# Macaron block on one core: the opening's stage order searched anew, up to about tile 13

## What is computed

```python
def _L0_ffn_ref(x, gate_w, w1, w2, w3):
    xf = x.reshape(-1, orig_shape[-1])
    scores = jnp.einsum('td,ed->te', xf, gate_w)
    probs = jax.nn.softmax(scores.astype(jnp.float32), axis=-1)
    weights, idx = jax.lax.top_k(probs, TOP_K)
    weights = weights / jnp.sum(weights, axis=-1, keepdims=True)
    x1 = jax.nn.silu(jnp.einsum('td,efd->tef', xf, w1))
    x3 = jnp.einsum('td,efd->tef', xf, w3)
    out_all = jnp.einsum('tef,edf->ted', x1 * x3, w2)
    expert_outs = jnp.take_along_axis(out_all, idx[:, :, None], axis=1)
    result = jnp.einsum('tkd,tk->td', expert_outs, weights)

x = x + 0.5 * _L0_ffn_ref(_layernorm(x), gate_w, w1, w2, w3)
x = x + _L0_attn_ref(_layernorm(x), W_q, W_k, gain, bias, log_mix, log_scale)
x = x + 0.5 * _L0_ffn_ref(_layernorm(x), gate_w, w1, w2, w3)
```

## Time and profile before

| | |
|---|---|
| three executions | 804.45, 806.5, 806.85 us; median 806.5 |
| the profiled execution | span 805.2 us from its first to its last instruction; the page gives no other time for it |
| TensorE busy | 695.8 us |
| VectorE, ScalarE, GpSimd busy | 561.3, 501.8, 451.6 us |
| granted TensorE clock, mean | 0.950 |

### The profile page before, as it was taken

How to read it: one execution, slowest core, us unless ns; L and a number is a source line. 1 busy time by engine, 2 the same in 40 slices (tenths; PEclk the granted TensorE clock), 3 DMA queues, 4 the chain that set the end, 5 groups by cost and what they waited for, 6 DMA issues and landing times.

```text
span 805.2 us, 17412 instructions
## 1 busy us (share of the span) xinstructions
PE 695.8 (86%) x4632; PEld 429.6 (53%) x4632; DVE 561.3 (70%) x1599; ACT 501.8 (62%) x975; POOL 451.6 (56%) x545
## 2 busy tenths in 40 slices
PE   1751458999999999999988999998999889999992
PEld 1641225566555665665555656655665555665652
DVE  6679782333687887889879898898865624335766
ACT  4647743353579895967779798977866324334431
POOL 3467878544443446567566645774676656453232
PEclk9875689999999999999999999999999999999997
DMA  8967476868796987888999898788988888699998
GB/s 337 426 221 162 116 211 179 164 134 143 170 206 126 180 159 149 199 160 172 168 171 197 173 192 168 149 186 135 186 158 178 162 201 144 128 164 212 236 246 320
DMA packets 318614, 150.75 MB, mean 187 GB/s; under 512 B 299133, under 2 KB 302589, under 8 KB 317757
## 3 DMA queue, kind: packets, MB, share of 16 engines
q1 hardware_dynamic: 300637, 111.98, 67.4%
q0 software_dynamic: 17888, 37.65, 16.7%
HBM read 33.96 MB, written 44.81 MB: 98 GB/s over the span
## 4 chain that ended last, share of the span: by engine, by line
PE 48%; DVE 18%; DMA 10%; issue 9%; ACT 6%; SPq 5%; POOL 3%; another core or an unknown queue 1%; POOLq 0%; ACTq 0%; DVEq 0%
PE B L1247 28%; PE B L1263 16%; DVE t_W L1557 2%; DMA yt<-t_W,t_idx 2%; DMA t_ph<-t_p 2%; DMA hs<-t_s,t_POS 2%; POOL hs L960 2%; DMA t_gh<-t_gp 2%; DVE t_s L1614 2%; DVE t_th L1755 1%; DMA t_W<-t_W 1%; PE B L1315 1%; PE B L1276 1%; SPq L1052 1%; DVE t_X L1775 1%
## 5 line engine op out<-in xcount | busy, mean ns | idle before, releaser
L1247 PE MATMUL B<-t_W,t_ht 128*128 x1704 | 398.9, 383 | 22.4 <-DVE t_W L1557 7.1
L1247 PEld LDWEIGHTS B<-t_W,t_ht 128*128 128x128 f16 x1704 | 166.8, 99 | 200.7 <-issue 35.8
L1755 DVE SCALAR_TENSOR_TENSOR t_th<-B,t_K,t_th 128x512 f32<-128x512 f32 x142 | 105.7, 747 | 115.9 <-PE B L1247 90.8
L1008 POOL DMA_INDIRECT yt<-t_W,t_idx x107 | 112.5, 1052 | 119.8 <-ACT t_W L1405 71.8
L1263 PE MATMUL B<-t_W,t_gh 128*128 x1284 | 160.7, 276 | 9.4 <-issue 6.4
L960 POOL DMA_INDIRECT hs<-t_s,t_POS x112 | 116.0, 1035 | 63.0 <-issue 29.0
L1263 PEld LDWEIGHTS B<-t_W,t_gh 128*128 128x128 f16 x1284 | 125.0, 99 | 43.2 <-issue 13.7
L1389 ACT ACTIVATE t_th<-B,t_K 128x512 f32<-128x512 f32 x142 | 96.8, 683 | 76.8 <-PE B L1247 49.1
L1398 ACT ACTIVATE t_gp<-t_th 128x512 f16<-128x512 f32 x107 | 66.2, 624 | 48.3 <-DVE t_th L1755 40.1
L1000 POOL DMA_DIRECT2D t_idx<-hs x142 | 80.1, 569 | 24.0 <-DMA yt<-t_W,t_idx 13.4
L1766 DVE TENSOR_TENSOR t_gp<-t_th,t_gp 128x512 f16<-128x512 f32 x107 | 75.0, 707 | 26.1 <-ACT t_gp L1398 21.3
(11 more groups left out here) (214 smaller groups left out, 898.2 us busy)
## 6 DMA issues: line engine op xcount, KB each, us to landing
t_W<-wk SPq DMA_DIRECT2D x6, 2048.0 KB, 17.6
t_hp<-yt SPq DMA_DIRECT2D x16, 512.0 KB
t_s<-yt SPq DMA_DIRECT2D x15, 512.0 KB
t_X<-x SPq DMA_DIRECT2D x8, 512.0 KB, 7.4
out<-t_X SPq DMA_DIRECT2D x7, 512.0 KB
t_ht<-hs SPq DMA_TRANSPOSE x142
t_idx<-hs POOLq DMA_DIRECT2D x142, 0.5 KB
hs<-t_ph SPq DMA_DIRECT2D x2, 952.0 KB, 5.0
```

The lines of the kernel that those rows point to most:

```text
L1008: eng.indirect_dma_start(yt_d[L], bass.IndirectOffsetOnAxis(ap=IDX[:, n % RING:n % RING + 1], axis=0), YO[n % YR], None).then_inc(d_y[n % ...
L1247: t = eng.matmul(B[b][:], HT[n % HTR][:, (2 * hl + db) * 128:(2 * hl + db) * 128 + 128], W16[:, bass.ds(expert[n] * 4096 + (db * 2048 + wl ...
L1755: eng.scalar_tensor_tensor(out=th[:], in0=B[b1][:], scalar=K[:, 7:8], in1=th[:], op0=ALU.mult, op1=ALU.mult).then_inc(free[b1], 1)
```

## The change

Only the string `ORDER` is changed: its first 459 stages, up to `ids 13`, `high 13` and the up halves of tile 14, are arranged anew; the 2662 behind them stand in the same order. The set of stages is the same, and so is each kind's own order but for `scatter`, `mark` and `rexp`. Since the three banks for the up halves are handed out in the order, they come to be permuted for all later tiles.

```diff
 ORDER = (
-    "))Bt)%)Bztf%efYeKY())BYY))BttLKL$$KLKL%$$++++qx%wpfeYKvY!!))fDLKL$$++eYYKLKL$++$Bt-^!!%f^!!e++>)q++xwp)Bt^+++++^"
-    "!!)YYz==+%)B??vV++++:$+ufe=Y=Y??t:$::%=?=?==!!fe^!!!^^!))?=B?$$=_!tY__Yqx??w==WW::uW??=p=+v$$%!1fe^!1!1!1?z?==Y^"
-    "^?Y:=:??==??;.;>;=N$^.?$S;qx!w~~~>;;.pP==!!uWWvD>-[~;NNSWQ}S.Whh??=?P!!1!1P^1QhVQ!1^1^=?M;W>;;|!1!1.NSs1>;~~.^E;"
-    "|>FNPyEN!1hQ!1|_SPuQ~^F;!1;!E>|.;SFE.F*PNW~;>;SQNPE.;>FE_~**W~SNSWP;.s1;>N;;S~uWQQWPca.FNS>;.;EQWW>F_;E~*Ns1FS*;"
+    "))Bt))%Bzt%f(eYfY))BeKLKYYtL)$%$KLK$L$)Btf)+)++%f+Bqx+wept%efv+YY++DKY!LK+!Y!$L$KLKLe++^!^^!$$!))++B-t++q!xY^:V+"
+    "wzp%Y:v=+++=++f!)?!)e?B+YY!=$$=?+?==?=u^!t!!+^?!:=):)^?=BW!Wu>W$%$qfxwpeY?tvY%Wz?=:$fe!1_:?!1$YY=?^=?~:$=?^^==?="
+    "?!1!1!1=^?:$q;x;!w>p!u.;!v^D?.!1!1;>NS=NS-[?!1^;;WW.N>s3P=PS!1h=?;?=?P^!1V.^;>;.;>NN=?!1;==??;.>N^!1!s1WSP;QS.;W"
+    ">QPEF!|QW||SP|~}NQS;EFP;hhE*>Qh;_.FE~y*___N*F~~Q.~u~~~*;EFEMN~WWS>;P_W._FSP*WuQQ*;NSP>;Wc.;>;;.>;.N;>NaSEs1WN~~F"
...
```

More of the change, by code:

```diff
@@ L133 @@
[L133 to L152, removed]
@@ new lines @@
+    "UU))BXF;;.>;QE*;~~t.WQuFWNS%IS>fNPPEe*YYJJW;;.S>;;>NUUUQ.PFU;;>))NBS.PTTWWW~*~~~~~QNEt%mFSonm&on/*___;Wu}Q;>Qf.P"
+    "<#;.&#NZ/E&#;GiSF~j<SeEW/Z<GFblYP&#ZYibGTj/N>;;>E.d;;>lTQP<CdNZi*_~*jmCl.GF~bobnmoSiA_E&n/*j;;ANF<SWW>PuPl#*dZ.&"
+    ";C/AQQQGQd~CA<i#SZEGFNjP*&;>OEWl/QW#&;r)b.FSiN)BSPPj;E#>;<t%.FfNJJUWWuSU.*;EP>;;>NQe.SWl/bZ;<PYFZU.GiQd;GEd>UNj*"
+    ")*;Q;_~C1Y:)Btb%l$F>NS.iNPEjFdQC:W*feE;l;bFSSYYP$ETTPqC>.Nxw;FE.QdCWF;N>puv*A1WQWSS~Amonmo&;;n#>P/P*A;*A_*&Or.<Z"
+    "/N.!GiE<^FQWQW;#WNZQ>;;>j~~~~~!!)&~ESSGPP.^/lQuW<N)#;FZ.iB;>&GSj/l<ENFSi!#ZG;;>~~.Ed1Pt%Pb1FfJJjUUd**N;;UU))S**."
@@ new lines @@
+    "b1PQEBtC1~A>;;>WlWWFi*b1.eEjYYd;QQFbC1EN%C.lWQ;d>SfeA1P;F.~YC*A1:NEFS:;YT*T$ENPSP*A$N>F;S.Oqx;Ewpv!r!N))BWtQPm>;"
+    ".onm~;>;~&SFEoP^%.Qu;f!n/~~~>#&<NN/ZQW;;>F^e#.!&*~~YYuWQJ;WW;>WN:JGiUU;ESPS.S<F#j/PlPQZ;$N.><E;***dZG&#GWF:iQQbU"
+    "U))BtjSul.E;P%*Ffe*$N/NW>qxYE;FC<.SAYw;>TTiEbjd;lp*F*S;P.QEZGWCviPNN!jmonmb1Fo&n/l~EQAQQSb#WF<d&!>ZCAd/^Gi<C;AjP"
+    "&SP.l;#>#;/O^ZN!Qr))!~Gi;>Bt**~~~d<jZ&/b.%EWWFSCfNJe;*E;>;WlJPUdY.F*Q;Y:UNbSGEUF.s2CU)P)B:uQ>;E*F#$i~NtjE$;>%.s<"
+    "FSfqEFexwsP;YpAQlWQvE;.**!!bFSZGiDA>dYPNS^TTCNEj;;>m.oW!^!-nlPmQ;;>bdASVNsoPFy1nC&S.E/AQ&F#uQWWWNP/<O<S**_~E#&r)"
@@ new lines @@
+    ")BZt;.;>;;>.NSF~**;EP%feJJ.uWWQWQ_NUPUYYSF;>;#;>E.UUNPG)ZSF;)ijNB;__E::.*G>$/*F<tPQQ;lWu$&E%fbqxZFw;>SQWijeNYEFp"
+    "G#**d;lPCEAY/b1..d;~<T>;*NvQSSFiENTS!ZjbGCPFPWmo~~~nmon&/lib;>;.jQWQ&#<.sN/;EZS^<P!Al#dNGiPCZ*j>&;Fd#WuG**.E/<Sb"
+    "CQlW&Zy2Q;>#AFi~~~^;dPAjO/yWlu<rZNGi)!j*WC)BGQ~~_lE;F.N>;d!ES;~~t~P*bb1>%FC;i.jEbfJWJUWUNUl.e;>dYN;;SPCSFS.dU**A"
+    "1AA>NCP)QW)BA*y1S;;Y.tEON:%uQ$>;;WQP:.Qr))WPNBtFf>;;e_ES.>YYFSPN;$;TT.E>;;F>P%Nfeqxw.QWWuWWQYEF***mYponv&mSSEon/"
+    "P~F~_*<~!;NPD&#::QQ.Z~~~!G;#>;;>E/&-S.^$;#$i!~b~PN~Wj<Z^FE!*NS;/.PqlQVF<Gi>;ZNdExw&;>pG.FSjCEPSAQWl#/biFjN*b<~;;"
@@ new lines @@
+    ".QZdSQ_C_*N**luGSi>EF;;WA~d>EPv.QjPFl;;>CENS.NSPPdbW;W;>;QWu**~FAC*.ANPO~~~WEQQQWr));.F>;N!~*BtES;>;SF!E.P%fWWeF"
+    "^NuY;>;.NYESF_;!EQPP.>;SP*FN::QW.;*^!>;N$$q**.SP;SE>;~;xwpQN.NFPWWvEQuQW~_S*PFS>;.;>D~N~~!*~~E;;>;F^E.P.S-[FEWWQ"
+    "NPQ;NSP*!^WQ|Vhhh!*|>E;;.NF!|Whu|*_F>;;Q>SQPEEQ.*NFSWP;.F;>;N._;EFEFE**QNWuWW>;;WSP~__S~__.NESPPS>;FF;.NPQSP_***"
+    "~~~~~~~~~QWQQ*~~>;.;>E;;WE>WN.SFPNSQQu;;>.FW*NSPP;.;>EF;NS;E>;.NS~~~**~F*~_;.WQWWPQEQuNP>;FE.FS**~~~;N>;;EE.>;PS"
+    "Fs;NSP~E*F*~PQW>;u.NSF*y1PQWE.F*~;>N~~EFSPQQ;EFWQW;>;.NS.;*PNSPQWuEEFF>;;>;.NSPQQWW;.NS~QEFEE~W***~P>;;>;FQF~**."
@@ L159 @@
+    "*N.;NSPSP>;;>E.NWJJ;;UUUF.SPNUJJWWQ>;;.NU~~Q~EF>;;SPUUUSJEu.WWs1NFQPy>;*.;SNS>E;;>JPU.EsQFFUUNSUWQPy1JQW;EgJEW;."
+    ">QP*UNS*F;;.>;;NS.PUPNuWEQQ>;;>W.F;;*>F**UUSNSPJPEEJg;]1QQ.NSUUUUg1.;FF']J*E*~NPg1yE,FFS]],**EEFF],P**g'EF]***'E"
+    "F*JUUUUJJUUUUJJJUUggUUggg")
 class Plan:
```

7 lines of the change are left out of this document (2 added, 5 removed).

## The result

The changed kernel took 808.64 us (median of 20 runs, 803.45 to 813.43), the kernel before 804.61 us (20 runs beside them, 799.1 to 811.57). The ratio is 1.0056, 95% interval 1.0038 to 1.0073: slower by some 4 us, where 798.0 and "faster" were forecast. The profiled execution had a time of 807.4 us, a span of 805.7 (before: 805.2) and a mean granted clock of 0.950.

What follows compares the result with a forecast made beforehand. GpSimd's queue up to the last fill was taken to set TensorE's hand-over at down 5; GpSimd and ScalarE's chain end together near 133, gaining 8.5 us: 798.0 from 806.5. Range 793.5 to 807; the forecast's own 794 to 800.5.

Steps and rivals of the forecast that it cites:

- Start of group 0, group 1 and group 2: GpSimd's first scatters of these groups: sooner by 1.3, 6.0 and 6.1 us, from earlier positions on VectorE.
- From group 2 to the last fill: GpSimd's stretch: six ids leave (minus 3.4 us), places 0 enters (1.0); last fill at 129.0, gain 8.5.
- rival C: GpSimd scatters between 53 and 129: more long ones beside VectorE's splits, mean 0.84 us each; 815 at 20 more; chance 0.15.
- Is TensorE there by 133?: ScalarE's marks through TensorE's downs: chain ready at 133.4, down 5 starts about 133.2 against 140.98.
- Behind the last fill: GpSimd's puts: put 0 at about 129.9, gain 7.9; down 5 3.15 us later as before, 133.0.
- First up half within 0.5 us: VectorE's split 15 at 90.4 against 90.05, so TensorE's first up half starts within 0.5 us of 90.39.
- The rest: From tile 14 on: same order, permuted PSUM banks cost 0, GpSimd carries no backlog on.
- A: Rival: ScalarE's marks decide; group 3's scatters gain nothing, down 4 at 138.4, gain 2.6 us (804); chance 0.20.
- B: Rival: gain given back as stalls move with the work or a later TensorE stage waits; 806; chance 0.13.

Runs made afterwards that it cites:

- e5: The kernel before, unchanged, run again with its own trace; ratio to before 0.999.
- e1: The changed kernel, unchanged, run once more; ratio to before 1.002.
- e13: Changed kernel with gt 3 and gt 4 ahead of the spare write and pads 1 to 3 on SyncE; ratio to before 1.0034.
- e8: Changed kernel with all writes that need no scatter (zero, spare, pads, fills) moved early; ratio to before 0.9947.
- e14: Changed kernel with zero and pads 1 to 3 early, spare left behind load 8, fills left last; ratio to before 0.9985.
- e10: Kernel before with PSUM banks 1, 2 and 7 changing places for the up-projections; ratio to before 0.9999.
- e4: Kernel before with only the spare write moved, behind load 8 on SyncE instead of behind gt 0; ratio to before 1.0043.
- e9: Kernel before with the writes that need no scatter moved early (zero, spare, line, pads, fills); ratio to before 1.0026.
- e6: Kernel before with GpSimd's queue alone in the changed kernel's order; ratio to before 1.0145.
- e15: Kernel before with TensorE's queue alone in the changed kernel's order; ratio to before 1.0053.
- e2: Changed kernel with SyncE's queue in the order of before, other four engines as changed; ratio to before 1.0035.

## Why the prediction was wrong, by its steps

- *Start of group 0, group 1 and group 2*: right in the first pair of traces (gains 1.0, 5.2 and 6.35 us against 1.3, 6.0 and 6.1), and there by the mechanism given: routing 1 came late in both (43.71 and 41.91), and the new queue had the positions ready by the time GpSimd wanted them. Where routing 1 is not late the mechanism has nothing to gain: e5 and e1 put the gains at 1.2 and 0.8 us for groups 1 and 2. The step took a wait of that trace for a part of the order.
- *From group 2 to the last fill*: 54.9 us against 53.4 forecast; in e1 50.05 against 56.2 in e5. The gain of the last fill was 7.3 us, and 7.0 in e1, against 8.5. That it came so near is partly luck: in the first trace the 3.4 us of waiting for group 3's positions, forecast as no wait, ate up what the moved `ids` gave; in e1 the missing gain of groups 1 and 2 was made up by fewer long scatters (four in this stretch, together 2.7 us over 0.96 each; in e5 seven and 5.6 us). The prediction's own 9.2 us of excess for the eleven long scatters add up to 8.3 from their durations, mean 0.76 and not 0.84; it moves rival C's price and not the forecast.
- *Is TensorE there by 133?* **This step failed first.** The sum followed ScalarE, VectorE and TensorE, and left out SyncE's queue, on which `spare` had moved from 106 to 121 and `pads` 1 to 3 between `gt 3` and `gt 5`. `down 4` ended at 135.4 in e1 instead of 133.4, after 4.5 us of waiting for `gt 4`. e13 and e8 show the cause: with the `gt`s ahead, or the writes early, it starts at 127 and ends before 129. In the first trace it ended at 141.1; there it was the hold told of below, and no wait for a `gt` shows.
- *Behind the last fill*: "`down 5` 3.15 us later as before". **Failed too.** It took the landing time of `put 0` as a constant. From `put 0` to `down 5` it was 10.7 us in the changed kernel and 9.5 in e1. In these two traces `evict 4` waits for `down 4`, so the landing is hidden behind the step above; e13 and e14 bring it out. The runs put in the constant's place: 1.5 us (e5, e10) or 1.7 (e8) without the burst of writes, 4.4 behind the spare write alone (e4), 6.4 behind it and the four fills (e14), and 6.4 with the pads as well (e13).
- *First up half within 0.5 us*: 89.35 against 90.39 in the first pair, but 89.65 against 85.18 in e1 and e5. So against a before whose routing 1 is not late this is a loss of 4.5 us at the start of the up-projections. The step had split 15 at 90.4 (it is over at 89.4 in e1), but compared it with a before that was itself late.
- *The rest*: from 143 on TensorE lost another 2.7 us of busy time in the first pair; banks cost nothing (e10), as said.
- Rivals: A was nearest by its symptom (fills near 129, `down 5` after 136). Its mechanism was there in part: in e1 ScalarE waits 3.9 us for landings in front of group 3's marks and TensorE 4.4 us for `tanh`, but what held `down 4` was `gt 4`. C was wrong: 7 scatters over 1.25 us where before had 11. B names "something that does not come sooner", but without a place and at no loss. What the outcome hung on, small transfers that land late behind large ones, was not among the rivals, though a DMA share of 0.97 stood in the earlier trace rows.

What stays open: the changed kernel's opening ends level with before's, and that explains 1.002 in e1. Of the 1.0056 in the first comparison it explains a part at most; the two intervals overlap, so it is open whether there is more to explain. What differs there are the late routing 1 and the holds below, which the later traces do not show in these places.

## What to carry to other kernels

When an order lets one engine finish sooner, ask what shares the transfer queues with its last commands: a landing time is no constant, in this kernel it grew from 1.5 to 6.4 us with the writes ahead of it. Try bulk writes that wait for nothing where the DMA share is low (e8; it did not help the old order, e9), and keep them, on an in-order queue, from between the small transfers that a busy engine waits for. One engine's order alone does not carry over into another order: e6 and e15 lost 1.45 and 0.53% that way, and e2 gained nothing.

## What I had not expected of the hardware

- A half-KB list took 5 us to land, and SyncE's transposes 2.7 to 3.1 us to issue instead of 1.2, at a DMA share of 1.09 (e1).
- In the changed kernel's first trace the engines that wait for TensorE are released late, three times. The matmuls of `down 0` are recorded as over at 122.2 and `evict 0` is released at 129.10, with 6.2 us of idle that the view can only call "issue". The counts of `rank 3` are over at 95.5 and the up half behind them at 96.9, and VectorE's positions of group 3 go at 99.65; this is GpSimd's wait of 3.4 us:

```profile
99.65 0.23 DVE L1681 TENSOR_TENSOR t_RK<-B,t_ebase 128x64 f32<-128x64 f32 x1 [6.30 <-remote]
```

 The third lies between 638 and 648, where the lead over before falls from 4.2 us at tile 106 to none at tile 109:

```profile
644.01 0.38 PE L1247 MATMUL B<-t_W,t_ht 128*128 x1 [0.16 <-issue]
645.42 0.38 PE L1247 MATMUL B<-t_W,t_ht 128*128 x1 [1.04 <-issue]
649.45 1.03 PE L1247 MATMUL B<-t_W,t_ht 128*128 x2 [3.65 <-DVE t_th L1755]
```

 The page warns that ends of matmuls are modelled. What holds them I did not find. e1, the same kernel, shows neither of the first two, so the order alone does not bring them about.
- One trace of the same order varies by 2.3 us at tile 15 (e5, e10) and by 5 us at group 2 between the first comparison and e5. Steps of 1 or 2 us should not be read from a single pair of traces.
